# Four consecutive tokens in a partition, and the residual of the fused stage kept in nine buffers

## The reference

```python
x = L0_attn_x                                   # (8, 1024, 256)
x = x + scan(_layernorm(x), W_dt, b_dt, W_B, W_C, A_log, D_param)
x = x + moe(_layernorm(x), gate_w, fc1_w, ..., s_fc1_w, ...)

# scan: 8 states for each of the 256 channels, over 1024 steps
dt = soft_clamp(softplus(x @ W_dt.T + b_dt), 0.001, 0.1, 0.5)
h  = h * exp(soft_clamp(dt * A, -8, 8, 0.5)) + (dt * x) * B      # every step
y  = sum_n h * C + D_param * x

# moe: 15 experts, the best 3 of a token, and a shared expert for all
scores = softmax(xt @ gate_w.T);  topk_w, topk_idx = top_k(scores, 3)
y_e = (gelu(g) * xh * geglu_mult) @ fc2_w[e].T + fc2_b[e]        # xh, g from fc1 of expert e
out = sum over the 3 of topk_w * y_e  +  shared expert (hidden width 512)
```

## Time and profile before

| | us |
|---|---|
| median of 3 runs | 1831.78 (1829.75 to 1833.33) |
| the profiled execution | 1826.3 |
| its span, first to last instruction | 1824.5 |
| stage 1, to the barrier | 149 |
| stage 2, the scan | 149 to 609 |
| stage 3, the fused stage, with set-up and drain | 610 to 1016 |
| stage 4, the experts | 1016 to 1666 |
| stage 5 | 1666 to 1824.5 |

### The profile page before, as it was taken

The page is one execution under the profiler, slowest core; times in us unless marked ns, Lnnn a source line. Parts: engine busy times, 40 slices in busy tenths (PEclk is TensorE's granted clock), DMA queues, the critical chain, the costliest instruction groups (busy, mean ns, idle before and its releaser), DMA issues. The chain is left out here.

```text
span 1824.5 us, 24494 instructions
## 1 busy us (share of the span) xinstructions
PE 1456.7 (80%) x5592; PEld 858.2 (47%) x5592; DVE 1082.2 (59%) x2159; ACT 872.9 (48%) x1490; POOL 1124.0 (62%) x1005
## 2 busy tenths in 40 slices
PE   6883676666666497769893599999999999995997
PEld 3332444334444243435452266666666666663564
DVE  5655999999999444225542244444444444441698
ACT  6887998989988222212220133333333333332210
POOL 6886887888887155546775366666666666662000
PEclk9996878998889698889997699999999999997998
DMA  4433233333332589999675122222222222235895
GB/s 136 134 117 130 82 115 127 124 98 124 105 116 69 189 113 133 101 139 139 85 96 73 43 88 89 87 87 87 88 89 88 87 87 88 88 89 181 283 349 204
DMA packets 130522, 216.48 MB, mean 119 GB/s; under 512 B 20694, under 2 KB 94422, under 8 KB 130416
## 3 DMA queue, kind: packets, MB, share of 16 engines
q1 hardware_dynamic: 94656, 133.23, 28.3%
q0 software_dynamic: 27904, 61.06, 10.8%
q10 hardware_dynamic: 7856, 20.86, 6.9%
HBM read 147.89 MB, written 67.21 MB: 118 GB/s over the span
## 5 line engine op out<-in xcount | busy, mean ns | idle before, releaser
L1761 PE MATMUL bank<-arena_dt,xgT 128*128 x832 | 394.0, 596 | 0.1
L738 POOL TENSOR_TENSOR state<-arena_x,b_all 128x1024 f32<-128x1024 f32 x128 | 300.9, 2362 | 66.6 <-issue 64.1
L762 PE MATMUL bank<-ident,state 128*128 128x128 f32 x1024 | 182.3, 311 | 169.0 <-ACT scaled L675 74.8
L1716 POOL DMA_INDIRECT choice_out<-ye,ids x208 | 204.7, 984 | 164.2 <-DVE ye L1869 160.8
L817 DVE TENSOR_TENSOR_SCAN state<-bank,state 128x1024 f32<-128x1024 f32 x128 | 291.8, 2281 | 5.0 <-POOL state L738 4.9
L1855 DVE TENSOR_TENSOR hid<-bank,arena_x 128x512 f32<-128x512 f32 x208 | 143.8, 692 | 250.7 <-PE bank L1761 250.7
L1313 POOL DMA_INDIRECT row_table<-choice_all,row_i x192 | 195.9, 1020 | 137.7 <-DMA row_table<-choice_all,row_i 58.2
L1707 POOL DMA_INDIRECT xg<-x_norm,tokens x208 | 200.7, 965 | 73.0 <-issue 61.0
L762 PEld LDWEIGHTS bank<-ident,state 128*128 128x128 f32 x1024 | 125.1, 157 | 231.4 <-DVE state L817 123.7
L1827 ACT ACTIVATE gluT<-bank 128x256 f32<-128x256 f32 x208 | 79.9, 384 | 321.9 <-PE bank L1770 320.4
L1778 PE MATMUL bank<-arena_x,gluT 128*128 x832 | 213.9, 380 | 0.0
(11 more groups left out here) (180 smaller groups left out, 2199.4 us busy)
## 6 DMA issues: line engine op xcount, KB each, us to landing
b_all<-bc_rows SPq DMA_DIRECT2D x64, 512.0 KB, 3.7
arena_x<-choice_out SPq DMA_DIRECT2D x64, 384.0 KB, 7.8
xin<-in_x SPq DMA_DIRECT2D x16, 512.0 KB
x_skip<-xin SPq DMA_DIRECT2D x16, 512.0 KB, 2.9
y_acc<-x_skip SPq DMA_DIRECT2D x8, 1024.0 KB, 7.4
x_mid<-y_acc SPq DMA_DIRECT2D x8, 1024.0 KB, 6.5
arena_x<-x_mid SPq DMA_DIRECT2D x16, 512.0 KB, 18.7
x_norm<-arena_x SPq DMA_DIRECT2D x16, 512.0 KB, 18.6
```

Of the source, the lines that this page charges most:

```text
L738: pool.tensor_tensor(state[j % STATES][:, :, here], gT[:, :, b, here], b_all[j % BUFS][:, here].unsqueeze(1).to_broadcast([P, KD, TH]), AL ...
L762: last = pe.transpose(bank[:, TURN + (BY_PE * j + q) % 2, i * D + k * P:i * D + (k + 1) * P], state[j % STATES][:, k, t * P:(t + 1) * P], ...
L1716: pool.indirect_dma_start(out=choice_out, out_offset=bass.IndirectOffsetOnAxis(ap=ids[:, j % 2, j // 2:j // 2 + 1], axis=0), in_=ye[c][:], ...
L1761: last = pe.matmul(bank[:, 2 + s, :], xgT[s][:, k, :], w1[:, k, ds(e_no * (2 * F), 2 * F)], start=(k == 0), stop=(k == KD - 1))
```

## The change

`group_rows` becomes "(p i) d -> p i d": token 4p + i of the group lies in partition p, place i, so that a partition's four rows are one run of 4 KB. `rows_of` of the scan follows (two runs of 4 KB a partition). Since xT is still in token order, the transposes of stage 1 write every fourth word of a PSUM row, and those of the scan and of the C values read every fourth word; in stage 3 the columns of a group stay in the order of the tiles, and only the number that is scattered for a token (`iota`) changes.

In stage 3 there are nine x2 buffers: the four of before, three in the space of b2, and two new ones in place of xm. The bias and the shared expert's output are added into the x2 buffer of the group, and it is stored from there. `load_xm` is gone. The load of group g into the buffer of group g - 9 waits for the store of that group's sum, if it has one, and else for its normalisation. Groups 0 to 5 are loaded at the start (before: 0 to 3 and two xm). b2 is loaded as one transfer in slot 36, after all x_norm stores; the four parts of b1 follow, with waits on ACT for the stores of the sums whose buffers they overwrite. In stage 5 a group's y3 is one transfer and not four.

```diff
     def group_rows(t, g):
-        return t[ds(g * (GT * P), GT * P), :].rearrange("(i p) d -> p i d", p=P)
+        return t[ds(g * (GT * P), GT * P), :].rearrange("(p i) d -> p i d", i=GT)
...
-                                last = pe.transpose(bank[:, 5 + k, i * P:(i + 1) * P], xn[s][:, i, k * P:(k + 1) * P],
+                                last = pe.transpose(bank[:, 5 + k, i:GT * P:GT], xn[s][:, i, k * P:(k + 1) * P],
                                                     ident[:])
...
-                            last = pe.transpose(bank[:, 7, i * 2 * N:(i + 1) * 2 * N], bc[c][:, i * P:(i + 1) * P],
+                            last = pe.transpose(bank[:, 7, i * 2 * N:(i + 1) * 2 * N], bc[c][:, i:GT * P:GT],
...
-                                    state[j % STATES][:, k, t * P:(t + 1) * P], ident[:])
+                                    state[j % STATES][:, k, t // GT * CH + t % GT:(t // GT + 1) * CH:GT], ident[:])
...
-                        return t[b * T:(b + 1) * T, :].rearrange("(i p) d -> p i d", p=P)
+                        return t[b * T:(b + 1) * T, :].rearrange("(h p i) d -> p h i d", p=P, i=GT)
...
-            xm = [sb(f"xm{c}", [P, GT, D]) for c in range(2)]
+            x2_own = [sb(f"x2_own{c}", [P, GT, D])[:] for c in range(2)]
+            x2 = [in_arena[2], in_b2[0], in_arena[3], x2_own[0], in_b2[1], x2_own[1], in_b2[2], in_arena[0], in_arena[1]]
...
                     def load_x2(g):
-                        sp.dma_start(x2[g % 4], group_rows(x_mid, g)).then_inc(x2_loaded[g % 4], 16)
+                        if g - NX in group_of[:G1]:
+                            sp.wait_ge(stored[group_of.index(g - NX)], 16)
+                        elif g >= NX:
+                            sp.wait_ge(xn2_made, g - NX + 1)
+                        sp.dma_start(x2[g % NX], group_rows(x_mid, g)).then_inc(x2_loaded[g % NX], 16)
...
-                    def load_xm(j):
-                        wait(sp, stored[j % 2], 16 * (j // 2))
-                        sp.dma_start(xm[j % 2][:], group_rows(x_mid, group_of[j])).then_inc(xm_loaded[j % 2], 16)
-
-                    def store_xm(j):
+                    def store_sum(j):
                         sp.wait_ge(acc_made, 2 * (j + 1))
-                        sp.dma_start(group_rows(x_mid, group_of[j]), xm[j % 2][:]).then_inc(stored[j % 2], 16)
+                        g = group_of[j]
+                        sp.dma_start(group_rows(x_mid, g), x2[g % NX]).then_inc(stored[j], 16)
...
-                    load_xm(0)
-                    load_xm(1)
+                    load_x2(4)
+                    load_x2(5)
                     for q in range(FIRST, LAST):
                         for g in routed_at(q):
                             store_xn2(g)
-                            if g + 4 < GROUPS:
+                            if 6 <= g + 4 < GROUPS:
                                 load_x2(g + 4)
                         j, i = q // KS, q % KS
                         if i == 2 and 1 <= j < G1:
-                            store_xm(j - 1)
-                        if i == 0 and 2 <= j < G1:
-                            load_xm(j)
-                    store_xm(G1 - 1)
+                            store_sum(j - 1)
+                    store_sum(G1 - 1)
...
                             act.dma_start(w2[:, :, at], w2_rows[:, :, at]).then_inc(w2_loaded, 16)
-                            act.dma_start(b2[:, at], b2_row[at].partition_broadcast(P)).then_inc(w_loaded, 16)
...
                                 act.wait_ge(xn2_stored[s], 8 * GROUPS)
+                            act.wait_ge(xn2_made, GROUPS)
+                            act.dma_start(b2[:], b2_row.partition_broadcast(P)).then_inc(w_loaded, 16)
+                            act.wait_ge(stored[group_of.index(8)], 16)
                             load_b1(0)
+                        if q == turn_slot(GROUPS - 1) + 4:
+                            act.wait_ge(stored[group_of.index(9)], 16)
+                            act.wait_ge(stored[group_of.index(11)], 16)
                             load_b1(1)
                             load_b1(2)
...
                     def add_bias(j):
-                        s = j % 2
-                        dve.wait_ge(xm_loaded[s], 16 * (j // 2 + 1))
-                        dve.tensor_tensor(xm[s][:], xm[s][:], sb2[:].unsqueeze(1).to_broadcast([P, GT, D]), ALU.add)\
+                        g = group_of[j]
+                        dve.wait_ge(xn2_made, g + 1)
+                        dve.tensor_tensor(x2[g % NX], x2[g % NX], sb2[:].unsqueeze(1).to_broadcast([P, GT, D]), ALU.add)\
                            .then_inc(bias_in, 1)
...
-                        for i in range(GT):
-                            t = group_of[g] * GT + i
-                            choices = choice_out[t * P * SLOTS:(t + 1) * P * SLOTS, :]
-                            sp.dma_start(y3[c][:, i, :],
-                                         choices.rearrange("(p k) d -> p (k d)", k=SLOTS)[:, 0:TOPK * D])\
-                              .then_inc(y3_loaded[c], 16)
+                        choices = choice_out[ds(group_of[g] * CH * SLOTS, CH * SLOTS), :]
+                        sp.dma_start(y3[c], choices.rearrange("(p i k) d -> p i (k d)", i=GT, k=SLOTS)[:, :, 0:TOPK * D])\
+                          .then_inc(y3_loaded[c], 16)
```

More of the change, by code:

```diff
@@ L862, in rows_of, with halves @@
                     def rows_of(t, b):
-                        return t[b * T:(b + 1) * T, :].rearrange("(i p) d -> p i d", p=P)
+                        return t[b * T:(b + 1) * T, :].rearrange("(h p i) d -> p h i d", p=P, i=GT)
+                    def halves(buf):
+                        return buf[:].rearrange("p (h i) d -> p h i d", i=GT)
                     def load(b):
                         wait(sp, acc_stored[b % 2], 16 * (b // 2))
-                        sp.dma_start(y_acc[b % 2][:], rows_of(x_skip, b)).then_inc(acc_loaded[b % 2], 16)
+                        sp.dma_start(halves(y_acc[b % 2]), rows_of(x_skip, b)).then_inc(acc_loaded[b % 2], 16)
                     def store(b):
@@ L871, in store @@
                         sp.wait_ge(sum_taken, (b + 1) * BY_ACT)
-                        sp.dma_start(rows_of(x_mid, b), y_acc[b % 2][:]).then_inc(acc_stored[b % 2], 16)
+                        sp.dma_start(rows_of(x_mid, b), halves(y_acc[b % 2])).then_inc(acc_stored[b % 2], 16)
                     def load_b(j):
@@ L1150, in model_kernel @@
             late, GD = KD * E * D, GT * D
-            x2 = [arena_x[:, late + c * GD:late + (c + 1) * GD].rearrange("p (i d) -> p i d", i=GT) for c in range(4)]
+            in_arena = [arena_x[:, late + c * GD:late + (c + 1) * GD].rearrange("p (i d) -> p i d", i=GT) for c in range(4)]
+            in_b2 = [b2[:, c * GD:(c + 1) * GD].rearrange("p (i d) -> p i d", i=GT) for c in range(3)]
             xn2 = [arena_x[:, late + (4 + c) * GD:late + (5 + c) * GD].rearrange("p (i d) -> p i d", i=GT)
@@ L1210, in model_kernel @@
             junk = sglu[1][:].rearrange("p k t -> p (k t)")[:, 0:RPP * P]
-            x2_loaded, xn2_stored, xm_loaded, stored = sems("x2_loaded", 4), sems("xn2_stored"), sems("xm_loaded"), sems("sh_stored")
+            NX = len(x2)
+            assert all(g not in group_of[:G1] for g in range(GROUPS - NX, GROUPS) if g % NX in (1, 4, 6))
+            x2_loaded, xn2_stored, stored = sems("x2_loaded", NX), sems("xn2_stored"), sems("sh_stored", G1)
             gate_loaded, s_loaded, w2_loaded, w_loaded, s_scaled, w_scaled = [sem(n) for n in (
@@ L1243, in model_kernel @@
             W1P, W2P, B1P = E * 2 * F // W1N, E * D // W2N, E * 2 * F // 4
-            W_LOADS = W1N + W2N + 4
+            W_LOADS = W1N + 1 + 4
             EH = (E + 1) // 2
@@ L1283, in _ @@
                         if i == 2 and 1 <= j < G1:
-                            store_xm(j - 1)
-                        if i == 0 and 2 <= j < G1:
-                            load_xm(j)
-                    store_xm(G1 - 1)
+                            store_sum(j - 1)
+                    store_sum(G1 - 1)
                     for s in range(2):
                         sp.wait_ge(xn2_stored[s], 8 * GROUPS)
-                        sp.wait_ge(stored[s], 8 * G1)
+                    for j in range(G1):
+                        sp.wait_ge(stored[j], 16)
                 @block.gpsimd
@@ L1323, in _ @@
                     rstds(1)
-                    pool.iota(choice_i, pattern=[[SLOTS * P, TILES], [1, TOPK]], base=0, channel_multiplier=SLOTS)                        .then_inc(consts_made, 1)
+                    pool.iota(ints[:].rearrange("p (g i k) -> p g i k", i=GT, k=TOPK),
+                              pattern=[[SLOTS * GT * P, GROUPS], [SLOTS, GT], [1, TOPK]], base=0,
+                              channel_multiplier=SLOTS * GT).then_inc(consts_made, 1)
                     pool.wait_ge(consts_made, 1)
@@ L1435, in normalise @@
                         c = g % 4
```

(17 more changed lines are left out.)

4 lines of the change are left out of this document (2 added, 2 removed).

## The result

| | before | after |
|---|---|---|
| median | 1833.2 (1828.9 to 1842.6, 20 runs) | 1823.7 (1815.4 to 1830.6, 20 runs) |
| ratio | | 0.9937, interval 0.9922 to 0.9953 |
| the profiled execution | 1826.3 | 1828.5 |

What follows compares the result with a forecast made beforehand. Five stages in turn, each with its own limit; in the fused stage POOL's chain of scatters is the path. Sum -24 - 2 + 3 - 1 - 4 = -28: 1798 against the profiled run, 1804 us against the median; range 1772 to 1838.

Steps and rivals of the forecast that it cites:

- First stage, -2: Layer norm and projections: xin loads and x_skip stores in 4 KB runs save 2 us, stepped PSUM writes cost nothing.
- Scan, +3: Scan: 1024 transposes load their stationary side from every fourth word, costing 3 us, with loads at 140 to 160 ns.
- rival (d): Stepped operands cost 25 us in the scan and 20 in the first stage: +14 in all, 1846 us; chance 0.14.
- Last stage, -4: Last stage: the second x_norm load, in 4 KB packets, lands sooner, so PE starts earlier, saving 4 us.
- POOL's wait for rows, -18.9: Fused stage: without the second x_mid read, POOL's 18.9 us wait for DVE's row numbers goes; bounds 0 and 18.9.
- Rival (c): Fused stage: loads behind stored sums hold DVE back and POOL starves as before; only -9, 1823 us; chance 0.10.
- POOL's landings, -5: Fused stage: POOL's 58.2 us of waits for earlier scatters to land fall by 5, taken between -37 and +21.
- the amount of the traffic (-37): Fused stage: scatter waits follow DMA load and fall by 37 us; as a rival 1772 us, chance 0.18.
- the length of its packets (+21): Fused stage: longer packets hold the scatters up, +21 us in place of -5; as a rival 1830 us, chance 0.15.
- SP's transfers at 6.5 us per MB: Fused stage: with 4 KB runs SP's queue pays 6.5 us per MB instead of 8.5, 116 us instead of 186.
- Forecast for the fused stage -24: Fused stage total: 18.9 us of waits for rows gone and 5 us off the waits for landings.
- Outside -4: Outside the fused stage: first stage -2, scan +3, between the stages -1, last stage -4.

Runs made afterwards that it cites:

- split: The changed kernel with 1 KB runs in the fused stage only, by interleaving buffer rows on the chip: 1822.25 us, 0.9928 (chip 1); 1834.67, 0.9939 (chip 2).
- the layout alone: The kernel before with only the 4 KB runs, their transposes, numbering and single y3 load, x_mid still read twice: 1878.42 us, 0.9969; again 1880.44, 0.998 (chip 4).
- stall: The changed kernel with 18 small powers on POOL (17.7 us) ahead of the scatters of group 8: 1872.71 us, 0.9943 (chip 4).
- the residual alone: The changed kernel with the old views, transposes, numbering and y3 loads (1 KB runs): 1861.75 us, 0.988, again 1863.95, 0.9893 (chip 4); 1831.34, 0.9905 (chip 2).
- after_d: The changed kernel itself, run again on chip 1 beside other variants: 1822.51 us, 0.9942.
- late: The changed kernel with all scatters put behind the last of POOL's 16 small norm chains: 2009.73 us (chip 3).

## Why the prediction was half right

- **First stage, -2: right.** 149.2 to 149.9 us in six profiles with the old view, 146.5 to 147.9 in fourteen with the new. The transposes into every fourth word of PSUM cost nothing, as counted: 298 ns each before and after. The Trainium skill's sentence on PSUM (Advanced Engine Details and Errata, Memory Cachelines) does not show here.
- **Scan, +3: the price was there, the cost wasn't.** The stationary load goes from 157 to 211 ns, between the 140 to 160 of the forecast and the 235 of rival (d):

```profile
L762 PEld LDWEIGHTS bank<-ident,state 128*128 128x128 f32 x1024 | 157.7, 211 | 199.3 <-DVE state L817 118.5 <-issue 77.2
```

  The Trainium skill's rule on SBUF lines (Advanced Engine Details and Errata, Memory Cachelines) fits that direction. But from the first stage's end to the fused stage's start it is 461.5 to 466.4 us in the six profiles with whole rows and 462.2 to 467.1 with stepped ones; rival (d) is out.
- **Last stage, -4: right, 6.** All six loads of xa land in 6.8 to 7.9 us, and PE's second turn starts 8.3 us after their issue, not 13.4 (before, 1680.38 - 1667.0):

```profile
1683.89 1.97 PE L200 MATMUL bank<-ident,xa_from 128*128 128x128 f32 x8 [2.62 <-DMA xa_from<-x_norm]
```

- **POOL's wait for rows, -18.9: right in size, its reason only in part shown.** With four tiles in flight it is gone, or under 3 us, in every profile with the nine buffers but one (8.0 us in `split`); with sixteen, where POOL runs ahead, 6 to 10 us are left. Where the nine buffers came alone the fused stage fell by 17 (chip 2) and 23 to 24 us (chip 4). But the wait is near gone in the layout alone too, and the stall says that such a wait is worth only a part of its length (7 of 18 us); the residual alone also moves 4.2 MB less, and no run parts the two. That -18.9 and -5 together came close to its 17 to 24 is in part luck. The loads behind stored sums did not put it back: one wait of DVE for a load was 15.7 us, over the 12 allowed, and POOL's queue of work covered it. Rival (c) had the right total, 1823, by another way.
- **POOL's landings, -5: this is the step that failed.** From 58.2 us they rose by 27 in the profile of after, and by 18 in that of `after_d`. The forecast put them between two causes, the amount of the traffic (-37) and the length of its packets (+21), each from one window, of 85 and 55 us, of one execution, and counted nothing for the new view of the tokens beyond its packets. Neither cause carries the rise. With 4.2 MB less to move they did not fall, and by the estimate from `late` about half of the wait or more would be there with no traffic at all. And packets of 1 KB and 3.6 KB wait alike. In its place the runs showed 14 to 15 us that the new view costs in this stage beside the nine buffers (chips 2 and 4; 3, within the noise, without them).
- **SP's transfers at 6.5 us per MB: wrong.** 8.3 stayed. The long packets were cheaper, by 2.5 us per MB in `split` against after, but with packets of 1 KB the changed kernel was dearer than the one before, 10.7 against 8.5 (chip 1), and the new view dearer than the old one, 10.3 against 9.1 (chip 2), one profile each. And most of the price is that of the scatters beside them: 2.6 without (chip 3).
- **Sum.** Forecast for the fused stage -24; measured -1 to -2 on the chip of the forecast, -7 on two others. Outside -4; measured -7 to -11.

What stays open: by which way the view of the tokens lengthens the landings and raises the transfers' price. The stage then reads and writes a partition's rows 1 KB and not 128 KB apart in main memory, and a scatter carries other tokens; no run held one of these fixed. Whether the residual alone is quicker on chip 1, that of the forecast, wasn't tried, nor were `late` and `stall`, so the 14 to 15 us are not shown there.

## What to carry over

Of a wait that a change removes, ask which limit of the same engine stands right behind it (here twelve scatters in flight) and test that limit first: sixteen tiles in flight gave 26 us on chip 1, more than the change itself. A DMA share near one beside scatters of single words can be the scatters' doing: put them off once, and read what the transfers cost alone. And a stage that differs by 50 us from chip to chip can't be priced from two windows of one execution.

## What the runs showed of the hardware

- Beside scatters of 128 words (some 70 in 180 us, 0.04 MB) the other transfers cost 9.8 and 10.2 us of engine share per MB, without them 2.6 and 3.1 (the changed kernel, with its scatters put off and not, one chip, one profile each).
- With at most twelve in flight and nothing beside them, scatters land one in 1.65 us, with 1.5% of the DMA engines busy.
- The length of the packets beside them makes no difference to the time with four tiles in flight and 39 us with sixteen. Per MB, SP's packets of 1 KB cost 10.7 us and those of 3.6 KB 8.2 (four tiles, the same view).
- The kernel before takes 411 us in the fused stage on one chip and 461 to 463 on two others, all else within 2.5 us. Most of the difference between two of its profiles, 405.6 and 466.1 us, is POOL's waits for landings (58.2 and 112.3).
